# Transposed projections in half-heads and scores in 32-row tiles, in a three-part decoder layer on one core

## The reference

```
x = x + attention(layernorm(x))          # 32 query heads, 8 key heads, width 64, causal, window 128, sinks
x = x + convolution(ctx, layernorm(x))   # long convolution over pair products
x = x + (sum over 8 factor matrices)(layernorm(x)) / sqrt(8) + bias
```

## Time and profile before

| | |
|---|---|
| median of 3 runs | 2218.97 us (2217.65 to 2219.78) |
| profiled execution, its own time | 2217.66 us |
| its span in the profile | 2215.5 us |
| PE busy | 2086.6 us (94% of the span) |
| DVE busy | 1753.5 us (79%) |
| ACT busy | 929.9 us (42%) |
| POOL busy | 835.2 us (38%) |
| granted clock of TensorE, mean | 0.977 of full speed |
| attention part | from 0 to 1717.5 us of the span |

### The profile page before, as it was taken

The page is one execution under the profiler, slowest core; times in us unless marked ns, Lnnn a source line. Parts: engine busy times, 40 slices in busy tenths (PEclk is TensorE's granted clock), DMA queues, the critical chain, the costliest instruction groups (busy, mean ns, idle before and its releaser), DMA issues. The chain is left out here.

```text
span 2215.5 us, 45127 instructions
## 1 busy us (share of the span) xinstructions
PE 2086.6 (94%) x12672; PEld 1656.8 (75%) x12672; DVE 1753.5 (79%) x6468; ACT 929.9 (42%) x3429; POOL 835.2 (38%) x1327
## 2 busy tenths in 40 slices
PE   5669999999999999999999999999998699999699
PEld 4557888888888888887777777777875577676587
DVE  6558887878888887777777787778776599999787
ACT  3334444444444444444444444444443122222233
POOL 3223333333344333333333333333331355454354
PEclk9889999999999999999999999999999899999899
DMA  7663111111111114311121111111101633233364
GB/s 232 187 188 116 49 61 55 64 60 48 48 48 48 48 65 180 115 39 49 50 76 49 49 48 49 61 54 48 49 30 48 231 84 90 83 91 83 111 219 160
DMA packets 84765, 191.72 MB, mean 87 GB/s; under 512 B 7777, under 2 KB 20833, under 8 KB 84465
## 3 DMA queue, kind: packets, MB, share of 16 engines
q1 hardware_dynamic: 72112, 157.67, 21.6%
q10 hardware_dynamic: 8640, 23.86, 2.9%
q0 software_dynamic: 3840, 8.39, 2.1%
HBM read 120.68 MB, written 60.90 MB: 82 GB/s over the span
## 5 line engine op out<-in xcount | busy, mean ns | idle before, releaser
L726 POOL TENSOR_TENSOR m<-qk,rope_sb 128x320 f32<-128x320 f32 x256 | 223.3, 872 | 956.9 <-DVE qk L826 956.9
L648 ACT ACTIVATE pr<-pr,mx 128x128 f32<-128x128 f32 x1024 | 399.3, 391 | 222.1 <-DVE mx L852 222.1
L486 PE MATMUL wP<-wh,xTh 128*128 128x384 f32 x1024 | 373.4, 365 | 10.5 <-DVE vv L829 10.5
L1091 PE MATMUL y<-kv,tap 128*128 128x288 f32 x1280 | 330.3, 414 | 27.3 <-DVE res L1139 9.6
L486 PE MATMUL wP<-wh,xTl 128*128 128x384 f32 x1024 | 353.3, 345 | 0.0
L486 PE MATMUL wP<-wl,xTh 128*128 128x384 f32 x1024 | 350.8, 343 | 0.0
L1091 PEld LDWEIGHTS y<-kv,tap 128*128 128x128 f32 x1280 | 240.6, 192 | 116.9 <-issue 25.1
L730 POOL TENSOR_TENSOR m<-qk,rope_sb 128x160 f32<-128x160 f32 x512 | 260.3, 530 | 0.0
L510 PE MATMUL sP<-qT 64*128 64x128 f32 (+1 forms) x2048 | 237.1, 350 | 1.0 <-DVE mx L852 1.0
L636 ACT COPY qT<-tP 128x384 f32<-128x384 f32 x256 | 122.6, 479 | 272.4 <-PE tP L496 272.0
L852 DVE CUSTOM_DVE_ANT_0 pr<-sP,mask_sb 128x128 f32<-128x128 f32 x1024 | 235.1, 284 | 0.7
(11 more groups left out here) (93 smaller groups left out, 3594.2 us busy)
## 6 DMA issues: line engine op xcount, KB each, us to landing
tap<-padded_taps SPq DMA_DIRECT2D x64, 256.0 KB, 3.4
kk<-in_ctxt SPq DMA_DIRECT2D x64, 192.0 KB, 3.1
x_in<-in_x SPq DMA_DIRECT2D x16, 512.0 KB, 4.9
fsum<-in_factors POOLq DMA_DIRECT2D x8, 1024.0 KB, 9.6
xb<-in_x SPq DMA_DIRECT2D x16, 512.0 KB, 4.3
xt_split<-xTh SPq DMA_DIRECT2D x16, 512.0 KB, 2.6
xt_split<-xTl SPq DMA_DIRECT2D x16, 512.0 KB, 3.7
x_part_rows<-x SPq DMA_DIRECT2D x16, 512.0 KB, 3.1
```

Source lines behind the costliest of these rows:

```text
L486: last = pe.matmul(wP[:, 0:GW], a[:, p // 4, j, c, :], w[:, g, c, :], start=(c == 0 and n == 0), stop=(c == KD - 1 and n == 2))
L648: act.activation(pr[:, s, a, cols], pr[:, s, a, cols], ACT.Exp, bias=mx[:, s, i:i + 1], scale=-1.0, accum_out=ac[:, s, i:i + 1])
L726: pool.tensor_tensor(m1[:, j], qk[:, j], rope_sb[:, j, 0], ALU.mult)
L1091: last = pe.matmul(y[:, s, c, 0:NY], tap[:, s, d * P:(d + 1) * P], kv[:, s, c - d, :], start=(d == 0), stop=(d == c))
```

## The change

The projection is turned over. The weights of a sweep are laid out in six **units** of 256 columns: the four keys together, four units with one query of each of the four key heads, and the four values together (`wh` and `wl` are now `[P, NU, KD, T]`). A unit is one call of `unit` on TensorE: 24 products of 256 columns to `wP`, with the weights as the stationary operand for queries and keys, so that they come out transposed, features on partitions and all 256 tokens along the row. The first 32 features of four heads are one half of `wP` and the second 32 the other half, so both halves of a head lie on the same partitions. A window's six units stand in slots 0, 1, 3, 5, 6 (the values) and 7.

The rotation follows: ScalarE copies the two halves crosswise, with the bias added, to `m2` (`bent`), VectorE takes (product + bias) * cos to `m1` (`turned`), GpSimd multiplies `m2` by the sines and adds `m1` (`rotate`: two instructions of 128 x 512 for each of five units). `q_transposes`, `q_evac`, `tP` and VectorE's `rotate` are gone. A head is now two pieces of 32 rows, so `scores` takes 16 products for four heads in every second slot, in four quarters of 32 rows, each summed over two products, to four banks. `out_projection` lags by a window or two and writes one bank `oP` for one tile and then the other, so each tile's first product waits for the residual sum that reads the bank. The x and x1 transposes use `wP`.

The weights of the second sweep are no longer stored in split form: they are loaded raw into `x_in` and `xn` when these are free and split at the joint, in ten pieces of 1024 columns (`split_now`), five of them in window 15, four in windows 16 and 17, one in window 18. The first sweep's are split in ten pieces in slots 0 to 7 of window 0 and ahead of it. The `fsum` transfers move from body 0 to body 1.

```diff
-                for c in range(KD):
-                    for n, (a, w) in enumerate(steps):
-                        last = pe.matmul(wP[:, 0:GW], a[:, p // 4, j, c, :], w[:, g, c, :],
-                                         start=(c == 0 and n == 0), stop=(c == KD - 1 and n == 2))
-                last.then_inc(qkv_done, 1)
...
+                    for h in range(2):
+                        for c in range(KD):
+                            for i, (w, a) in enumerate(steps):
+                                last = pe.matmul(wP[:, h * T:(h + 1) * T], w[:, n, c, h * P:(h + 1) * P], a[:, s, c, :],
+                                                 start=(c == 0 and i == 0), stop=(c == KD - 1 and i == 2))
+                    last.then_inc(qk_done, 1)
+
+            def scores(y, p):
+
+                v = y.window(p - 2)
+                g = 8 * y.m + p - 2
+                pe.wait_ge(qr_ready, (QM + 1) * v + (p - 2) % 4 + 2)
+                wait(pe, masked, 2 * g)
+                kslot = ((p - 2) // 4) % 2
                 for t in range(NT):
-                    for a in range(2):
-                        r = slice(a * HD, a * HD + HD)
-                        k0 = t * P
-                        last = pe.matmul(sP[:, a, k0:P + 2 * k0], qT[r, s, j, t * P:(t + 1) * P],
-                                         qT[r, s, 2, 0:(t + 1) * P], start=True, stop=True)
+                    for h in range(2):
+                        for r in range(GS):
+                            rr = slice(r * 32, r * 32 + 32)
+                            last = pe.matmul(sP[:, r, t * P:P + 2 * t * P], qT[rr, p % 2, h, t * P:(t + 1) * P],
+                                             kT[rr, kslot, h, 0:(t + 1) * P], start=(h == 0), stop=(h == 1))
                 last.then_inc(s_done, 1)
...
+                if k == 0:
+                    wait(pe, x1_ready, 2 * v + t)
...
+            def bent(y, p, i):
+                v = y.window(p)
+                s = (p // 4 + i) % 2
+                act.wait_ge(qk_done, (QM + 1) * v + i + 1)
+                wait(act, qr_ready, (QM + 1) * v + i - 1)
+                for half in range(2):
+                    last = act.activation(m2[:, s, 1 - half], wP[:, half * T:(half + 1) * T], ACT.Identity,
+                                          bias=bqk_sb[:, y.sweep, i, half:half + 1])
+                last.then_inc(bent_ready, 1)
...
+                pool.tensor_tensor(m2[:, s], m2[:, s], rope_sb[:, 1 if i == 0 else 0, 1:3], ALU.mult).then_inc(sin_ready, 1)
...
+                pool.tensor_tensor(dst, m1[:, s], m2[:, s], ALU.add).then_inc(qr_ready, 1)
...
-                    if y.first:
-
+                    if y.number == 1:
                         if p > 0:
                             pool.wait_ge(f_in, 16 * p)
                             pool.dma_start(fsum[:], factors[p], accum_op=ALU.add, max_dma_last_dim=4 * D).then_inc(f_in, 16)
...
+                for half in range(2):
+                    last = dve.scalar_tensor_tensor(m1[:, s, half], wP[:, half * T:(half + 1) * T], bias[:, half:half + 1],
+                                                    tab[:, 0], ALU.add, ALU.mult)
+                last.then_inc(m_ready, 1)
```

More of the change, by code:

```diff
@@ L284, in here, with window @@
                 return not (self.first and n < 0) and not (self.drain and n >= 0)
-            def old_sweep(self):
-                return 0 if self.joint else self.sweep
+            def window(self, p):
+                return 2 * self.m + p // 4
         def bodies(eng, body):
@@ new lines, in unit @@
+                if (y.first or y.joint) and p < 4:
+                    pe.wait_ge(lo_done, NS * y.sweep + n + 1)
+                unit_free(y, p, n)
+                steps = [(wh, xTh), (wh, xTl), (wl, xTh)]
+                if n == V_UNIT:
+                    for t in range(NT):
+                        for c in range(KD):
+                            for i, (w, a) in enumerate(steps):
+                                last = pe.matmul(wP[:, t * T:(t + 1) * T], a[:, s, c, t * P:(t + 1) * P], w[:, n, c, :],
+                                                 start=(c == 0 and i == 0), stop=(c == KD - 1 and i == 2))
+                    last.then_inc(v_done, 1)
+                else:
+                    for h in range(2):
+                        for c in range(KD):
+                            for i, (w, a) in enumerate(steps):
+                                last = pe.matmul(wP[:, h * T:(h + 1) * T], w[:, n, c, h * P:(h + 1) * P], a[:, s, c, :],
+                                                 start=(c == 0 and i == 0), stop=(c == KD - 1 and i == 2))
+                    last.then_inc(qk_done, 1)
@@ new lines, in out_projection, with out_here @@
+                if k == 0:
+                    wait(pe, x1_ready, 2 * v + t)
+                steps = [(oTh, woh), (oTl, woh), (oTh, wol)]
+                for c in (2 * k, 2 * k + 1):
+                    for n, (a, w) in enumerate(steps):
+                        last = pe.matmul(oP[:], a[:, o, c, t * P:(t + 1) * P], w[:, c, :],
+                                         start=(c == 0 and n == 0), stop=(c == NO - 1 and n == 2))
+                last.then_inc(out_done, 1)
+            def out_here(y, p, j):
+                last_slot = p % 4 == 3 and j == 1
+                if y.first:
+                    return p == 7 and j == 1
+                return not (y.drain and p == 7 and j == 1)
@@ L573, in body @@
+            for t in range(NT):
+                x_transposes(0, t)
             def body(y):
@@ L1351, in _, with decoder_layer @@
             steps(dve, body, lag=4)
-def decoder_layer(nc, x, ctxt, wqkv, bqkv, wout, bout, sinks, ssm_pad, dcoef, factors, bias, rope, masks, ident, out):
+def decoder_layer(nc, x, ctxt, wqkv, bqk, bv, wout, bout, sinks, ssm_pad, dcoef, factors, bias, rope, masks, ident, out):
     x1_dram = nc.dram_tensor("x1_rows", [B, T, D], F32).ap()
```

794 lines of the change are left out of this document (378 added, 416 removed).

## The result

The changed kernel takes 2186.1 us (2185.5 to 2186.3, four runs) against 2218.6 (2217.7 to 2219.8, four runs) for the kernel before: a ratio of 0.985, 95% interval 0.984 to 0.987, so 32.5 us less. The forecast was 113 less, 2106, and the result lies 1 us outside its range. The profiled execution took 2186.3 us, its span is 2184.5.

What follows compares the result with a forecast made beforehand. TensorE was taken to bound the middle, transfers and dependent splits the first two to three windows. Start -59, windows 4 to 15 -17, windows 16 to 30 -59, joint +20, end +2: together -113, 2106 us as median, range 2065 to 2185.

Steps and rivals of the forecast that it cites:

- TensorE's terms: TensorE's list per window: units +0.3, queries' transposes -3.4, scores -0.9, so 50.1 becomes 46.1 us.
- factor of 3.07: Skill's speed-up for four 32-row tiles: scores would take 1.67 us, against the 1.50 taken with quarters side by side.
- The loop of VectorE and ScalarE: Masks, exponentials, `den` to `pT`: 4.88 us a slot; 47.1 us a window in the first sweep, 46.1 in the second.
- the inverse root ahead of the sinks: Slot 0, first sweep: the inverse root waits for the layer norm ahead of the sinks, adding 1.6 us to the loop.
- Waits: TensorE waits 1.3 us at transposes of x in the first sweep, 0.8 or 0.9 a window for the residual sum.
- the window was taken to repeat without a seam: Windows 4 to 15 at 48.7 us each, -17; windows 16 to 30 at 47.0, -59.
- The start: Fewer transfers: window 4 starts at 199 us instead of 258.5, -59; rival of only 20 gained, chance 0.09.
- At the joint +20: Splits in windows 15 to 17: 10 pieces at about 2 us each, in line with the loop, +20.
- some 42 us: Window 0's work, six units plus two short slots and splits: some 42 us from 13.
- The rival "GpSimd holds VectorE up": Each rotation holds `den` or the division by 0.6 us: +65, 2170; chance 0.17, with a small tail above.
- The rule named beside that rival: Skill: plain two-input elementwise work belongs on VectorE, GpSimd about 2 times slower; by it the rotation should slow the kernel.
- The end: Seven projections of 1.49 us stand alone behind the last pairs: 96 us against 94.3, +2.

Runs made afterwards that it cites:

- experiment 8: Combined: changed kernel with loops written out, ScalarE's split half ahead of the exponentials, residual sums ahead save the first tile's in the first sweep: 2106.1 us.
- experiment 1: Changed kernel with both loops over bodies written out in all lists: 31 us less, 2155.1 us.
- experiment 2: Changed kernel with the layer norm's inverse root behind the sinks on GpSimd: 2188.7 us, no gain.
- 5: Changed kernel with two bodies (four windows) to an iteration, the fifth body written out: 22.8 us less.
- 6: Kernel before the change with its two loops over bodies written out: ratio 0.9997 (0.9988 to 1.0007).
- 11 to 14: Changed kernel, loops written out in TensorE's list alone (8 us less), VectorE's alone (nothing), both (31.6 less); kernel before, two bodies an iteration (same within interval).
- experiment 9: Combined kernel (2106) with GpSimd's output bias one slot earlier and the residual sum ahead everywhere: 2094.1 us.
- experiment 4: Changed kernel with ScalarE's half of a weight split ahead of the exponentials of its slot: 22.6 us less.
- experiment 7: Written-out changed kernel (2155) with GpSimd's rotation passes cut to 8 columns, so the rotation is left out: 15 us less.
- experiment 10: Kernel with the output bias one slot earlier (2094.1), first tile of `xn` moved between `mask_transposed` and `turned`: 11 us slower.
- 3: Changed kernel with the residual sum ahead of the division on VectorE and the second layer norm behind the masks: 6.5 us less.
- 13: Changed kernel with the loops written out in VectorE's list alone: nothing gained.

## Why the prediction was wrong, point by point

- **TensorE's terms: right, with 0.6 us a window missing.** Unit products 0.12 apart, a unit 3.02 us (1436.98 to 1440.00) for 2.97, scores 1.52 for 1.50. The bare list is 46.7 us (experiment 8) for 46.1; 0.3 of the difference are the six units, 0.3 I did not place. Over windows 18 to 30 that is 8 of the 30 us missed there. The 1.67 us that the prediction worked out from the Trainium skill's factor of 3.07 are not borne out at these sizes.
- **The loop of VectorE and ScalarE: its pieces right, wrong in one use.** In experiment 1 it is 3.07 us from the masks to the next `den` (312.53 to 315.60) for 3.08, and 1.20 and 0.60 as forecast. Not in the sum was VectorE's wait for ScalarE's copy ahead of `turned`, 0.81 us in slot 7. The loop was given 1.6 us for the inverse root ahead of the sinks; experiment 2 shows that this order did not set the period.
- **Waits: one right, one too small.** For the transposes of x 1.3 us a window was forecast, 1.1 measured (experiment 8, 12.3 over 11 windows). For the residual sum the forecast was 0.9 in the second sweep, and the wait itself was 1.0 (experiment 1, 12.2 us over 12 windows). But the units' wait for `turned`, put at nothing, was another 0.3 (4.0 over 12), and moving the sum away won 1.6 a window in all (48.3 to 46.7). So the waits of the second sweep were short by 0.7, 9 us over 13 windows.
- **The step that failed most: the window was taken to repeat without a seam.** The period was put together from slots, with no term for the jump back, since the rows of before show windows of 50.19 inside and outside the loop alike. They do in the first sweep, because the pause of VectorE (2.90 us in the row above) lay in slack and TensorE's branch took 0.2. The change took away the slack and made TensorE's pass longer. It costs 31 us in windows 4 to 30, shown by experiments 1, 5, 6 and 11 to 14; an estimated 7 to 9 of them are the lower clock behind the pauses, which the prediction did not have either. The prediction asked of the slots what is late next, but not of the place between two bodies.
- **The start: the splits were priced at the joint but not there, and the clock nowhere.** At the joint +20 was forecast for about 2 us a piece in line with the loop, and windows 15 to 17 took 165.6 us against 163. The sum came out, but in part by luck: experiment 4 takes 12.8 of it off by order, and the granted clock is 0.96 there, where the same windows had 1.00 before and have 1.00 again in experiment 9 (143.4 us). The same pieces in window 0 were put into "some 42 us", which was 53.3. Experiment 4 takes 10.9 off the start by order alone. The 7 us that stay are 4 in window 0, 1.3 in windows 2 and 3, whose period was too short, and the rest ahead of and in window 1. In window 0 the clock is 0.84, and all terms of the forecast come from rows at full clock although has 0.87 and 0.93 for the start. This is an untested candidate for the 4 us; the rotation beside the splits is another, since experiment 7 took 4.1 off the start.
- **The rival "GpSimd holds VectorE up": present, but small here.** The rotation costs 15 us at most (experiment 7), none of it in the steady windows of the first sweep. Instructions did get long: 23 of the 256 `den` took 0.77 to 1.23 us for a median of 0.16, but only 8 of them beside the rotation, 15 beside the output bias. In the steady windows of the first sweep it is one a window, in line ahead of a residual sum for which TensorE waits 1.1 us. The prediction had 0.4 us for this; the row is 0.8 longer than the median, so by my estimate up to 0.8 us a window come of it. No run tested it apart. The rival's +65 needed that each of them be in line. Experiment 10 shows what it costs when one is. The rule named beside that rival, that two-input work belongs on VectorE, would have had the rotation slow the kernel. It costs these 15 us at most; no run moved it to VectorE, so which engine is the better place stays open.
- **The end: +2 forecast, +8.2 measured.** 3.7 of it went with the combined order (108.0); the rest was not looked into.

Not tried: `turned` beside `bent`, which would take the wait for ScalarE's copy out of VectorE's list. Both read the same bank of PSUM, and the kernel orders them.

Add the parts that were removed: 31.0 (jump back) and 22.6 (splits) leave 2132.5; the residual sum in the second sweep and the rest of experiment 8 take off 26.4, at 2106.1. That this is the forecast number is in part chance: the start is 6 us later than forecast there and the joint 10 us shorter.

Of the 80 us, then, 31 are the jumps, 18 the start, 5 the first sweep and 17 the second sweep apart from the jumps, 3 the joint and 6 the end.

## What to carry to other kernels

When a change turns an engine with slack into one without, look at the seams of its loops too, and at the trace for what each engine does just behind its branch; a pause that costs nothing today is the first bill after the change. Two pauses at the same place hide each other: taking away either gives little, so an experiment on one alone can acquit both. And a half of a two-engine job belongs where its own engine waits, not where the code of the other half stands: changes of order alone won 61 us (2155.1 to 2094.1) beyond the 31 of the loops, without changing what is computed. Last, a pause of TensorE can cost more than its length: look at the distance of the products behind it.

## What the runs showed of the hardware

- A taken branch at the end of a pass: VectorE's next instruction starts 3.0 to 3.3 us behind it in the first sweep of the kernel before and 4.7 to 5.1 in the second, and 3.6 to 3.9 and 4.4 to 5.7 in the changed kernel. Part of this would be waiting in any case: in experiment 1 `den` waits 1.48 at this place. TensorE's branch is 0.2 us in the kernel before, with 672 matrix records a pass (3363 in ten windows) and as many loads, and 3.5 to 4.4 us in the changed one, with 848 (4668 in eleven windows; 3.3 to 6.5 in experiments 2, 3, 4 and 13); with two bodies to a pass it is 3.7 to 4.3 in both. Where between 672 and 848 it turns was not tried. Behind these rows stands the Trainium skill, "Runtime: NRT & Kernel Launch", section "Instruction fetch mechanics": a taken branch whose target is outside the window held on the engine forces a fetch before execution goes on, and TensorE's store is four times as large as the others'. The trace agrees in kind: VectorE pays in both kernels and TensorE only with the longer pass. That the pause is a fetch is the page's account; what the runs show is that the length of TensorE's pass decides. The page's sizes, 2048 instructions for TensorE and 512 for the others, do not tell the cases apart: by the trace's records a pass has 1463 instructions of TensorE before and 1789 after, and 506 and 452 of VectorE. The section gives no duration; the rows have 3.5 to 4.4 us for TensorE's branch.
- TensorE's clock: behind each pause of 2.5 to 2.8 us at a jump of the first sweep the granted clock was at its lower level, and products of 256 columns started 0.21 us apart instead of 0.12. With the loops written out the clock of windows 4 to 14 is 1.00.
- Beside a rotation, a normalisation of 128x512 on VectorE took 1.48 us instead of 0.54, and `den` with its two small operands 1.23 instead of 0.16. Beside the output bias they took 1.63 and 1.0. The Trainium skill, "SBUF — State Buffer", section "SBUF: two separate sides", says that the port pair shared by VectorE and GpSimd is an exclusive lock for a whole instruction, and names VectorE instructions with two inputs from SBUF, as `den` is, among those that take it. The trace agrees in kind: `xn` starts 0.1 us behind the rotation and ends 0.3 behind its end. It does not agree to the letter, since `xn` alone takes 0.54; the rows of GpSimd are rough.
